# A mixture-of-experts pipeline with every handoff between engines a whole round apart, eight result buffers and scatters held for one round

## The chip, the core and the metric

The kernel runs on one core of one Trainium2 chip. The metric is the device time of the whole program in microseconds (us), median of several runs. The engines are TensorE (PE in the rows; PEld is its loading of weights), VectorE (DVE), ScalarE (ACT), GpSimd (POOL) and SyncE (SP, which here only issues DMAs).

## The reference

A small transformer block in float32 on `x` of shape (4, 256, 256). First `x` gets the result of a grouped-query attention (16 heads, 4 key/value heads, width 128, a causal mask and a learned bias) whose input is a gated bidirectional scan over the side input. Then `x` gets the result of a mixture of experts whose input is a second such scan `h`, flattened to 1024 tokens of width 256:

```python
logits = x @ gate_weight.T                       # 64 experts
routing_weights, selected = top_k(softmax(logits), 8)
routing_weights /= routing_weights.sum(-1)
for each expert e:
    gate, up = split(x @ gate_up_weights[e])     # 256 -> 2 x 96
    out = (silu(gate) * up) @ down_weights[e]    # 96 -> 256
    final += combine[:, e] * out
```

Each token goes to 8 of the 64 experts, so there are 8192 pairs of token and expert.

## The kernel before

The first some 320 us (attention, both scans, routing) are not touched by the change. At their end GpSimd has scattered each token's row of `h`, with its routing weight and its pair number, into a table in HBM (`slot_rows`), grouped by expert. What follows is the expert pipeline, then a fold that adds the eight results of every token.

**Tiles.** The pipeline works on 96 *doubles*. A double is 128 rows: two tiles of 64 rows, each with its own expert. The 32 fixed doubles cover the first 64 rows of every expert (expert 2j in the upper half, 2j+1 in the lower). The 64 extra doubles (28 to 91 in the order of work) take the rows beyond 64 of the experts that have them. Their experts are known only at run time, so their weights are read at an offset in a register, and those of the lower half are first copied to fixed places (`copy_gu` by VectorE, `copy_dn` by ScalarE).

**Groups and rounds.** Doubles 0 to 3 are groups of their own; from there on a group is two doubles and shares PSUM banks and evacuations. There are 50 groups. `ROUNDS` lists what a round works on: groups 0 to 3 singly, then two groups (four doubles) a round. There are NR = 27 rounds, of which 23 are full.

**The stages of a group**, with the semaphore that each hands on (in brackets):

1. SP loads the double's rows from `slot_rows` into one of ten `xrow` buffers, two DMAs a double (`rows_ld`). It may do so once VectorE has read the double ten before (`dest_ready`).
2. TensorE transposes the rows, `turn_rows` (`xt_done`); VectorE copies them from PSUM to `xg`, `copy_turned_rows` (`xt_copied`), and works out the weight column `wcol` and the row numbers `dest`, `find_rows` (`dest_ready`).
3. TensorE multiplies by the gate and up weights, `gate_up`, L1685 (`gu_done`).
4. ScalarE takes silu of the gate half into `sact`, `silu`, L833 (`silu_done`); VectorE multiplies by the up half and the routing weight into `aact`, `weigh`, L1323 (`act_ready`).
5. TensorE transposes `aact`, `turn_act` (`at_done`); ScalarE copies it to `aT`, `copy_turned` (`at_copied`).
6. TensorE multiplies by the down weights, `down`, L1706 (`dn_done`); ScalarE copies the result to `eout`, `copy_out` (`out_copied`).
7. GpSimd scatters `eout` to `pair_rows` in HBM with one indirect DMA for each double, L620 (`scattered[i]`, one semaphore for each of the six result buffers).

Every engine is in order, and each has its order written out by hand. In round `g` the orders are, where (g) stands for the groups of round g:

- TensorE: `turn_rows` (g), `turn_act` (g-2), `gate_up` (g-1), `down` (g-2).
- ScalarE: `copy_turned` (g-2), `silu` (g-1), `copy_out` (g-2), `copy_down` (g-1).
- VectorE: `copy_turned_rows` and `find_rows` (g), then `weigh` (g-1) and `copy_gate_up` (g) in turn, group by group.
- GpSimd follows `out_copied`, double by double.

So `weigh` of round g-2 ends while TensorE is near the end of its round g-1, and `turn_act` wants it after the eight transposes that begin round g; and `aT` is copied while TensorE does the `gate_up` that stands between `turn_act` and `down`. `sact` is one buffer: the second `silu` of a round waits for the first `weigh` (`act_ready`). The `gate_up` results use PSUM banks 2 and 3 in turn, the turned activations banks 4 and 5. Bank 5 is also used once, in round 5 (`TABLE_AT`), to turn the table of the extra doubles.

**The fold.** When the scatters have landed, SP loads `pair_rows` in eight slices of 1 MB (two DMAs each) into `pairs`, L472. VectorE adds half of each and TensorE the other half. Slices 0 and 1 wait for all scatters but those of the last three doubles:

```python
last = NDBL - TOPK // 2 + r // 2
for i in range(NOUT) if r == 0 else [last % NOUT]:
    sp.wait_ge(scattered[i], 16 * len(range(i, last + 1, NOUT)))
```

The functions that the change touches, and their callers:

## Time and profile before

| | |
|---|---|
| time, median of 3 runs | 521.24 us (520.41 to 523.81) |
| span of the profiled execution | 576.6 us |
| instructions in it | 10371 |
| TensorE busy in the span | 477.4 us (83%) |
| VectorE, ScalarE, GpSimd busy | 342.7, 305.9, 212.3 us |
| mean granted TensorE clock | 0.947 of full |

The profiled execution is 55.4 us longer than the median of the timed runs, with the same instructions. No time of its own is given for it beside its span. Starts in the rows are microseconds from the start of that span; durations of matmuls are modelled, their starts are recorded. The pipeline's full rounds lie between about 360 and 542 us of it.

### The profile page before, as it was taken

Reading aid. Unit: us, or ns where it says so; the run is one execution under the profiler, and the core shown is the slowest. Engines: PE = TensorE matmul, PEld = TensorE weight load, DVE = VectorE, ACT = ScalarE, POOL = GpSimd, SP = SyncE. Lnnn points to the kernel's source line nnn. Section 1 sums busy time; section 2 is a strip of 40 time slices with the busy share of each in tenths; the row PEclk is TensorE's granted clock in tenths of the full one; section 3 lists DMA queues with packets and bytes.
Section 4 is the critical chain, followed back from the end, with each engine's and each line's share of the span. In section 5 each row is a group of like instructions: output and inputs, shape, how many; then the busy total and the mean of one; then the engine's idle time right before and its main releaser. Section 6 shows DMA issues by size and latency. Waiting matters only on the chain. (4 is left out here: it accounts for less than half of the span.)

```text
span 576.6 us, 10371 instructions
## 1 busy us (share of the span) xinstructions
PE 477.4 (83%) x3073; PEld 351.1 (61%) x3073; DVE 342.7 (59%) x1204; ACT 305.9 (53%) x854; POOL 212.3 (37%) x224
## 2 busy tenths in 40 slices
PE   4586999999899899999983766987988888888666
PEld 1366767877787678788653423765665666655322
DVE  4768496596685894795793564544355454553033
ACT  3456787885966887779864201333244343444200
POOL 0344110041114631025584642245444455445600
PEclk9799999999999999999996788999899899899879
DMA  8920862000301102002998739884444444330097
GB/s 283 411 70 19 167 131 74 1 1 0 76 1 54 69 30 73 2 1 74 345 404 291 278 107 298 227 288 129 111 115 115 113 128 127 107 95 13 19 363 304
DMA packets 47318, 79.49 MB, mean 138 GB/s; under 512 B 8266, under 2 KB 31127, under 8 KB 46880
## 3 DMA queue, kind: packets, MB, share of 16 engines
q1 hardware_dynamic: 36864, 55.34, 31.1%
q0 software_dynamic: 7680, 16.93, 8.2%
q10 hardware_dynamic: 2720, 6.55, 3.5%
q8 instruction: 26, 0.43, 0.3%
q14 instruction: 28, 0.23, 0.1%
HBM read 56.54 MB, written 26.44 MB: 144 GB/s over the span
## 5 line engine op out<-in xcount | busy, mean ns | idle before, releaser
L620 POOL DMA_INDIRECT pair_rows<-eout,dest x93 | 91.8, 987 | 99.5 <-ACT eout L634 78.2
L833 ACT ACTIVATE sact<-ps 128x192 f32<-128x192 f32 (+1 forms) x50 | 16.3, 325 | 122.7 <-remote 73.6
L1323 DVE SCALAR_TENSOR_TENSOR aact<-sact,wcol,ps 128x96 f32<-128x96 f32 x96 | 26.0, 311 | 92.6 <-issue 87.1
L1685 PE MATMUL ps<-wts,xg 128*64 (+1 forms) x512 | 71.5, 342 | 3.7 <-DVE copy_gu L1346 2.2
L691 ACT ACTIVATE lg<-lg,mneg 128x128 f32<-128x128 f32 (+1 forms) x128 | 56.4, 443 | 26.1 <-DVE mneg L1029 21.5
L1685 PEld LDWEIGHTS ps<-wts,xg 128*64 128x64 f32 x512 | 53.0, 143 | 16.5 <-issue 9.5
L541 POOL DMA_INDIRECT slot_rows<-rows,pair_slot x48 | 47.9, 998 | 37.2 <-issue 24.1
L1512 PE MATMUL ps<-oT,wo_sb 128*128 128x256 f32 x240 | 54.4, 380 | 0.0
L1706 PE MATMUL ps<-wts,aT 96*64 96x256 f32 (+1 forms) x256 | 49.8, 395 | 4.4 <-issue 3.4
L1512 PEld LDWEIGHTS ps<-oT,wo_sb 128*128 128x128 f32 x240 | 44.6, 190 | 6.2 <-ACT oT L634 0.7
L634 ACT ACTIVATE lg<-lg,rinv 128x128 f32<-128x128 f32 (+1 forms) x128 | 45.9, 448 | 2.5 <-issue 1.7
L1685 PE MATMUL ps<-copy_gu,xg 128*64 128x192 f32 x256 | 46.6, 337 | 0.0
L1029 DVE CUSTOM_DVE_ANT_0 lg<-ps,bm 128x128 f32<-128x128 f32 (+1 forms) x128 | 36.9, 352 | 11.3 <-PE ps L1468 9.5
L1306 DVE COPY xg<-ps 128x512 f32<-128x512 f32 (+1 forms) x50 | 33.2, 664 | 15.4 <-PE ps L1387 8.8
L1387 PE MATMUL ps<-ident,xrow 128*128 128x128 f32 x192 | 31.0, 294 | 12.1 <-DMA xrow<-slot_rows 6.8
L1387 PEld LDWEIGHTS ps<-ident,xrow 128*128 128x128 f32 x192 | 22.3, 149 | 28.6 <-issue 21.2
L1383 PE MATMUL ps<-hh,wqh 128*128 128x256 f32 x128 | 38.1, 298 | 1.6 <-DVE kl L988 1.6
L1706 PE MATMUL ps<-copy_dn,aT 96*64 96x256 f32 x128 | 33.9, 385 | 6.4 <-issue 6.4
L1706 PEld LDWEIGHTS ps<-wts,aT 96*64 96x64 f32 x256 | 27.3, 141 | 15.8 <-issue 4.8
L1384 PE MATMUL ps<-hl,wqh 128*128 128x256 f32 x128 | 36.7, 287 | 0.0
L1385 PE MATMUL ps<-hh,wql 128*128 128x256 f32 x128 | 36.7, 287 | 0.0
L501 POOL TENSOR_TENSOR eukv<-euk,vT 128x512 f32<-128x512 f32 x8 | 10.2, 1273 | 67.1 <-ACT euk L669 50.6
(237 smaller groups left out, 1184.4 us busy)
## 6 DMA issues: line engine op xcount, KB each, us to landing
wts<-in_experts_dram SPq DMA_DIRECT2D x22, 640.0 KB, 8.0
xrow<-slot_rows SPq DMA_DIRECT2D x192, 65.0 KB
pairs<-pair_rows SPq DMA_DIRECT2D x16, 512.0 KB, 11.2
wts<-in_experts_dram ACTq DMA_DIRECT2D x10, 640.0 KB, 6.1
slot_rows<-zero SPq DMA_DIRECT2D x1, 4160.0 KB, 24.2
wT<-in_wq_t_dram SPq DMA_DIRECT2D x4, 512.0 KB, 6.5
wq_raw<-in_wq_l_dram SPq DMA_DIRECT2D x1, 2048.0 KB, 14.6
wo_sb<-in_wo_l_dram SPq DMA_DIRECT2D x1, 2048.0 KB, 20.5
```

The costliest lines, as they stand in the source:

```text
L541: nc.gpsimd.indirect_dma_start(out=slot_d, out_offset=bass.IndirectOffsetOnAxis(ap=pair_slot[:, t, k:k + 1], axis=0), in_=r[:, k, :], in_o ...
L620: nc.gpsimd.indirect_dma_start(out=pair_d, out_offset=bass.IndirectOffsetOnAxis(ap=dest[:, d:d + 1], axis=0), in_=out_rows(d), in_offset=N ...
L634: copy = lambda o_, i_, s=1.0: nc.scalar.activation(o_, i_, ACT.Copy, scale=s)
L691: ins = nc.scalar.activation(t, t, ACT.Exp, bias=mneg[:, u % 2, c:c + 1], scale=-1.0, accum_out=rsum[:, u % 2, c:c + 1])
L1029: ins = V.tensor_tensor_reduce(t, s, m, 1.0, FLT_BIG, ALU.add, ALU.min, mneg[:, u % 2, c:c + 1])
L1383: nc.tensor.matmul(o_, a[0], b_[0], start=start, stop=False)
L1384: nc.tensor.matmul(o_, a[0], b_[1], start=False, stop=False)
L1385: return nc.tensor.matmul(o_, a[1], b_[0], start=False, stop=stop)
L1387: T_ = lambda o_, i_, n=P: nc.tensor.transpose(o_, i_, ident[0:n, 0:n])
L1512: ins = nc.tensor.matmul(ps[:, 7, m * T:(m + 1) * T], wo_sb[:, n * G + h, m * P:(m + 1) * P], oT[:, h, :], start=(n == 0 and m == 0 and h ...
L1685: ins = nc.tensor.matmul(ps[h * R:(h + 1) * R, 2 + u % 2, k * I2:(k + 1) * I2], xg[u % len(xg)][:, k, cc, h * R:(h + 1) * R], moving, star ...
L1706: ins = nc.tensor.matmul(ps[h * R:(h + 1) * R, 6 + a % 2, k * C:(k + 1) * C], aT[a % 2][0:I, k, h * R:(h + 1) * R], moving, start=True, st ...
```

## The change

It alters only the expert pipeline.

- **TensorE** in round g: `turn_rows` (g) and `gate_up` (g-1) in turn, group by group; then `turn_act` (g-2); then `down` (g-3). The loop has one round more (NR + 3).
- **ScalarE** in round g: `silu` (g-1), `copy_turned` (g-2), `copy_down` (g-2), `copy_out` (g-3). `copy_turned` waits for both groups of its round.
- **VectorE** in round g: for each group `copy_turned_rows` and `copy_gate_up` (g), then `weigh` (g-1); both `find_rows` (g) at the end.
- **Buffers**: `sact` gets a second buffer; from group 8 on `gate_up` cycles through the three banks 5, 2, 3; both groups' turned activations share bank 4; the result buffers are eight (four pairs) and not six.
- **GpSimd**: in rounds 4 to 23 (`PACED`) the first scatter of round r waits until the down products of round r+1 are done.

```diff
-    NOUT = 6
+    NOUT = 8
@@
-        sact = at("sact", [P, 2, I], take(2 * I * 4))
+        sact = [at(f"sact{i}", [P, 2, I], off) for i, off in enumerate((take(2 * I * 4), row_off + 2 * KIB))]
@@
-        eout = at("eout", [P, NOUT, C], rows_off[0])
+        eout_pair = [at(f"eout{i}", [P, 2, C], off) for i, off in enumerate([rows_off[0] + 2 * i * KIB for i in range(NOUT // 2 - 1)] + [row_off])]
@@
+        PLAIN = 8
+        def gu_bank(u):
+            return 2 + u % 2 if u < PLAIN else (5, 2, 3)[(u - PLAIN) % 3]
+        def gu_before(u):
+            return u - 2 if u < PLAIN else u - 3
+        PACED = range(TOPK // 2, NR - 3)
@@ GpSimd
             for d in range(NDBL):
+                r = round_of[group_of[d]]
+                if r in PACED and group_of[d] == ROUNDS[r][0]:
+                    pool.wait_ge(dn_done, ROUNDS[r + 1][-1] + 1)
                 pool.wait_ge(out_copied, group_of[d] + 1)
@@ ScalarE, copy_turned and silu
-                act.wait_ge(at_done, a + 1)
+                act.wait_ge(at_done, ROUNDS[round_of[a]][-1] + 1)
@@
-                if u >= 1:
-                    act.wait_ge(act_ready, u)
+                if u >= 2:
+                    act.wait_ge(act_ready, u - 1)
@@ ScalarE, the loop
-            for g in range(NR + 2):
+            for g in range(NR + 3):
                 us = ROUNDS[g - 1] if 1 <= g <= NR else []
-                outs = ROUNDS[g - 2] if g >= 2 else []
-                for a in outs:
-                    copy_turned(a)
+                outs = ROUNDS[g - 2] if 2 <= g < NR + 2 else []
                 for u in us:
                     silu(u)
                 for a in outs:
+                    copy_turned(a)
+                for a in outs:
+                    copy_down(a)
+                for a in ROUNDS[g - 3] if g >= 3 else []:
                     copy_out(a)
-                for u in us:
-                    copy_down(u)
@@ VectorE, the loop
-                for x in ins_:
-                    copy_turned_rows(x)
-                    find_rows(x)
                 us = ROUNDS[g - 1] if g else []
                 for k in range(max(len(us), len(ins_))):
+                    if k < len(ins_):
+                        copy_turned_rows(ins_[k])
+                        copy_gate_up(ins_[k])
                     if k < len(us):
                         dve.wait_ge(dest_ready, us[k] + 1)
                         weigh(us[k])
-                    if k < len(ins_):
-                        copy_gate_up(ins_[k])
+                for x in ins_:
+                    find_rows(x)
@@ TensorE, turn_act and gate_up
-                if a >= 2:
-                    pe.wait_ge(at_copied, a - 1)
-                if a == TABLE_AT:
-                    pe.wait_ge(cols_read, 2)
+                if a == ROUNDS[round_of[a]][0] and a:
+                    pe.wait_ge(at_copied, a)
@@
-                if u >= 2:
-                    pe.wait_ge(act_ready, u - 1)
+                if u == PLAIN:
+                    pe.wait_ge(cols_read, 2)
+                if gu_before(u) >= 0:
+                    pe.wait_ge(act_ready, gu_before(u) + 1)
@@ TensorE, the loop
-            for g in range(NR + 2):
-                outs = ROUNDS[g - 2] if g >= 2 else []
+            for g in range(NR + 3):
                 if g < len(IDLE):
                     keep_clock(IDLE[g])
-                for x in ROUNDS[g] if g < NR else []:
-                    turn_rows(x)
-                for a in outs:
+                xs = ROUNDS[g] if g < NR else []
+                us = ROUNDS[g - 1] if 1 <= g <= NR else []
+                for k in range(max(len(xs), len(us))):
+                    if k < len(xs):
+                        turn_rows(xs[k])
+                    if k < len(us):
+                        gate_up(us[k])
+                for a in ROUNDS[g - 2] if 2 <= g < NR + 2 else []:
                     turn_act(a)
-                for u in ROUNDS[g - 1] if 1 <= g <= NR else []:
-                    gate_up(u)
-                for a in outs:
+                for a in ROUNDS[g - 3] if g >= 3 else []:
                     down(a)
```

## Rows read from the trace of the kernel before

**Rows 1.** The page: span, and TensorE's busy tenths in 40 slices

```profile
span 576.6 us, 10371 instructions
PE   4586999999899899999983766987988888888666
```

**Rows 2.** Stretches: us, then busy us of PE, PEld, DVE, ACT, POOL; clock; DMA share; GB/s

```profile
410.00:508.50 98.50, 84.00 (x721) 60.09 (x722) 49.14 (x216) 40.83 (x121) 47.47 (x48) 0.97 0.43 119
...
544.50:577.00 32.50, 18.06 (x33) 6.24 (x32) 9.80 (x8) 1.19 (x2) 3.94 (x4) 0.89 0.80 303
```

**Rows 3.** Groups of instructions in 410.0 to 508.5 us: busy, mean ns, idle before

```profile
L620 POOL DMA_INDIRECT pair_rows<-eout,dest x48 | 47.5, 989 | 51.3 <-ACT eout L634 40.3 <-issue 11.0
L1323 DVE SCALAR_TENSOR_TENSOR aact<-sact,wcol,ps 128x96 f32<-128x96 f32 x48 | 12.9, 311 | 47.8 <-issue 47.8
L833 ACT ACTIVATE sact<-ps 128x192 f32<-128x192 f32 x25 | 8.3, 331 | 57.4 <-remote 32.9 <-PE ps L1685 9.6 <-issue 8.4
```

**Rows 4.** Timeline of round 6 and the start of 7 (TensorE, then ScalarE): start, us, what, idle before

```profile
365.01 1.04 PE L1387 MATMUL ps<-ident,xrow 128*128 128x128 f32 x8
366.94 2.82 PE L1685 MATMUL ps<-wts,xg 128*64 128x192 f32 x32
369.60 1.90 PE L1706 MATMUL ps<-wts,aT 96*64 96x256 f32 x16
371.43 1.09 PE L1387 MATMUL ps<-ident,xrow 128*128 128x128 f32 x8
...
368.51 0.33 ACT L833 ACTIVATE sact<-ps 128x192 f32<-128x192 f32 x1 [1.08 <-PE ps L1685]
```

**Rows 5.** Timeline of round 20 by engine: TensorE, ScalarE, VectorE

```profile
475.03 1.09 PE L1387 MATMUL ps<-ident,xrow 128*128 128x128 f32 x8
475.96 0.60 PE L1387 MATMUL ps<-ident,aact 128*96 128x128 f32 x4
...
479.14 0.38 PE L1706 MATMUL ps<-wts,aT 96*64 x1
...
481.14 0.33 PE L1387 MATMUL ps<-ident,xrow 128*128 128x128 f32 x1
...
477.35 0.65 ACT L634 ACTIVATE aT<-ps 96x256 f32<-96x256 f32 x2
480.80 0.33 ACT L833 ACTIVATE sact<-ps 128x192 f32<-128x192 f32 x1 [2.80 <-PE ps L1685]
...
481.21 0.54 DVE L1323 SCALAR_TENSOR_TENSOR aact<-sact,wcol,ps 128x96 f32<-128x96 f32 x2 [2.82 <-issue]
```

**Rows 6.** Round 20's gate and up products alone: us, PE busy, PEld busy

```profile
476.49:479.14 2.65, 2.65 (x32) 2.21 (x32) 1.00 0.37 97
```

**Rows 7.** Timeline of GpSimd from 522 us: the scatters of rounds 23 to 26

```profile
524.89 0.98 POOL L620 DMA_INDIRECT pair_rows<-eout,dest  x1 [2.50 <-ACT eout L634]
532.24 0.98 POOL L620 DMA_INDIRECT pair_rows<-eout,dest  x1 [2.50 <-ACT eout L634]
...
539.34 0.98 POOL L620 DMA_INDIRECT pair_rows<-eout,dest  x1 [2.25 <-ACT eout L634]
...
544.50 0.98 POOL L620 DMA_INDIRECT pair_rows<-eout,dest  x1 [0.30 <-issue]
...
548.37 0.98 POOL L620 DMA_INDIRECT pair_rows<-eout,dest  x1 [0.30 <-issue]
```

**Rows 8.** Timeline from 522 us: SP's queue, then TensorE's start of round 26

```profile
547.08 10.13 SPq L472 DMA_DIRECT2D pairs<-pair_rows  x16
...
522.28 0.55 PE L1387 MATMUL ps<-ident,xrow 128*128 128x128 f32 x3
```

**Rows 9.** The chain that ended last: the last scatter's landing

```profile
547.08 6.20 DMA pair_rows<-eout,dest
```

**Rows 10.** Waits of SP's queue in 395 to 545 us: total, times, longest

```profile
SPq L429 <- DVE dest L1314: 10.1, 6, 2.7
```

**Rows 11.** Timeline of TensorE in the single rounds

```profile
354.05 0.44 PE L1387 MATMUL ps<-ident,xrow 128*128 128x128 f32 x2 [2.38 <-DMA xrow<-slot_rows]
```

More of the change, by code:

```diff
@@ L214, in adaln_attn_ffn @@
         o = 16 * KIB
-        xg = [at(f"xg{i}", [P, 2, CC, P], off) for i, off in enumerate((take(2 * KIB), take(2 * KIB), r3 + 10 * KIB, rows_off[0] + NOUT * KIB))]
+        xg = [at(f"xg{i}", [P, 2, CC, P], off) for i, off in enumerate((take(2 * KIB), take(2 * KIB), r3 + 10 * KIB, rows_off[0] + (NOUT - 2) * KIB))]
         wcol = at("wcol", [P, (NE + MORE) // 2], take(384))
-        sact = at("sact", [P, 2, I], take(2 * I * 4))
+        sact = [at(f"sact{i}", [P, 2, I], off) for i, off in enumerate((take(2 * I * 4), row_off + 2 * KIB))]
         aact0 = take(2 * I * 4)
@@ L358, in adaln_attn_ffn @@
         NR = len(ROUNDS)
+        round_of = {g: r for r, gs in enumerate(ROUNDS) for g in gs}
         TABLE_AT = 5
@@ L830, in silu @@
                 act.wait_ge(gu_done, u + 1)
-                if u >= 1:
-                    act.wait_ge(act_ready, u)
-                nc.scalar.activation(sact[:, 0:n, :], ps[:, 2 + u % 2, 0:n * I2].rearrange("p (k i) -> p k i", k=n)[:, :, 0:I],
+                if u >= 2:
+                    act.wait_ge(act_ready, u - 1)
+                nc.scalar.activation(sact[u % 2][:, 0:n, :], ps[:, gu_bank(u), 0:n * I2].rearrange("p (k i) -> p k i", k=n)[:, :, 0:I],
                                      ACT.Silu).then_inc(silu_done, 1)
@@ L845, in copy_out @@
                 else:
-                    copy(eout[:, d % NOUT:d % NOUT + n, :], ps[:, 6 + a % 2, 0:n * C].rearrange("p (k c) -> p k c", k=n)
+                    copy(eout_pair[d % NOUT // 2][:], ps[:, 6 + a % 2, 0:n * C].rearrange("p (k c) -> p k c", k=n)
                          ).then_inc(out_copied, 1)
@@ L1322, in weigh @@
                 for k, d in enumerate(GROUPS[u]):
-                    ins = V.scalar_tensor_tensor(out=aact[u % 2][:, k, :], in0=sact[:, k, :], scalar=wcol[:, d:d + 1],
-                                                 in1=ps[:, 2 + u % 2, k * I2 + I:(k + 1) * I2], op0=ALU.mult, op1=ALU.mult)
+                    ins = V.scalar_tensor_tensor(out=aact[u % 2][:, k, :], in0=sact[u % 2][:, k, :], scalar=wcol[:, d:d + 1],
+                                                 in1=ps[:, gu_bank(u), k * I2 + I:(k + 1) * I2], op0=ALU.mult, op1=ALU.mult)
                 ins.then_inc(act_ready, 1)
@@ L1684, in gate_up @@
                                 moving = copy_gu[m % NCOPY][:, cc * I2:(cc + 1) * I2]
-                            ins = nc.tensor.matmul(ps[h * R:(h + 1) * R, 2 + u % 2, k * I2:(k + 1) * I2],
+                            ins = nc.tensor.matmul(ps[h * R:(h + 1) * R, gu_bank(u), k * I2:(k + 1) * I2],
                                                    xg[u % len(xg)][:, k, cc, h * R:(h + 1) * R], moving, start=(cc == 0), stop=(cc == CC - 1))
```

7 lines of the change are left out of this document (3 added, 4 removed).

## The prediction

> **What bounds the kernel now.** The page comes first: in the pipeline's part of the span, from slice 26 on, TensorE is busy eight to nine tenths, a little less than before it [rows 1]. The stretches put numbers to it. Twelve full rounds with extra experts take 98.5 us, so 8.21 us each; in them TensorE is busy 84.0 / 12 = 7.0 us, VectorE 4.1, ScalarE 3.4, GpSimd 4.0 [rows 2]. From the start of round 6 (365.01) to that of round 26 (522.28) there are 20 rounds in 157.3 us, 7.86 each [rows 4, 8]. No other engine comes near that time, so what can be won is TensorE's own waiting.
>
> How long must a round be? Rounds 6 and 20 give the pieces by their starts: eight row transposes 475.03 to 475.96, 0.93 us; four transposes of activations to 476.49, 0.53; 32 gate and up records 2.65; 16 down records 479.14 to 481.14, 2.00 (1.83 in round 6, 369.60 to the next start at 371.43). Together 5.9 to 6.1 us [rows 4 to 6]. So the profiled round holds 7.86 - 6.0 = 1.9 us of stall, and over the 20 rounds and the last ones (21 in all) that is 39 us. This is the most that a better order can give.
>
> Then I asked what the stall is. In round 6 silu begins at 368.51, 1.57 us after `gate_up` began (366.94): half of the 2.82 us, plus a hop [rows 4]. In round 20 the same silu begins at 480.80, 4.31 us after 476.49, though ScalarE had been idle 2.80 us and the products had the same length; the releaser named is the product itself [rows 5, 6]. The matmul is recorded as run and its signal comes some 2.9 us late. VectorE then idles as long (2.82 us before L1323), which is where nearly all of its 47.8 us at that line and ScalarE's 57.4 at L833 come from [rows 3, 5]. So the handoff that is late in this trace is the completion of a dense run of matmuls, and not `turn_act` waiting for a slow VectorE.
>
> Is that lateness there when nobody records? The recorder writes every instruction, and a full round has 60 matmul and 60 weight-load records, the densest stretch of the program. The profiled execution is 55.4 us longer than the median. If the timed rounds take 6.1 us, 21 x 1.75 = 37 us of it lie here, and 18 are left for the rest. If the timed rounds were as long as the profiled ones, all 55 us would have to come out of the other 410, much of which TensorE fills to eight or nine tenths [rows 1]. I take the first: in the timed runs a round is already about 6.1 us, and TensorE is nearly full. This is argued, not seen, and it is the largest choice here.
>
> **The change part by part.** *Order of TensorE, `sact`, banks.* These take the short handoffs away: `turn_act` no longer waits for the second `weigh`, `gate_up` waits for an `act_ready` one group older, the two silus do not wait for each other. Worth: between 0 (no stall in a timed round) and 1.9 us a round. Would a round of 6.0 us have stalled before? With TensorE at t = 0: the gate and up products of the first group end at 0.93 + 0.53 + 1.33 = 2.8, silu takes 0.33 and `weigh` 0.54 with hops of about 0.25, so 4.2; the second silu can go at 4.5, its `weigh` ends by 5.7; `turn_act` wants it at 6.0 + 0.93 = 6.9. Slack 1.2 us. The copy to `aT` (0.65) starts at 1.8 and `down` wants it at 4.1: slack 1.6. VectorE's 4.1 us and ScalarE's 3.4 fit in 6.0. So I put the saving in a timed round at 0.1 to 0.15 us, for rounds that a late DMA or a fall of the clock (0.97 in the extra rounds) [rows 2] puts out of step: 21 x 0.13 = 2.7 us, bounds 0 and 39.
>
> *VectorE's order.* The four `find_rows` pairs move behind both `weigh`, about 2.5 us later. SP is queued behind them: its loads wait for `dest_ready`. Today that wait is 10.1 us in six places over some 18 rounds [rows 10], and SP's eight DMAs a round run about a round ahead of their use (round 20's are issued while round 18 runs). The 2.5 us come out of that lead: 0, or up to 0.3 us a round if SP falls behind, 6 us.
>
> *ScalarE's order.* `copy_down` waits for the down products four doubles back, then `copy_out` for dn_done and for scatters two rounds old; silu of the next round is queued behind both. It has a round of slack now: 0.
>
> *Filling the pipeline.* In rounds 1 to 5 TensorE waits for the rows' DMAs (2.38 us at 354.05) [rows 11], and the stage that is one round deeper hides there: 0, bound 1 us.
>
> *The hold and the deeper drain.* This has a price that I can count. Before, the scatters of round r follow `down` (r), which TensorE does in its round r+2. After, `down` (r) is in round r+3 and its scatters wait for `down` (r+1), in round r+4: two rounds later. In the middle nothing waits for them (the eight buffers see to it), but GpSimd is the last to finish, and it can't catch up: an indirect DMA holds it for (548.37 - 544.50) / 3 = 1.29 us, 5.16 us a round [rows 7]. At the end of TensorE's round 26 GpSimd before starts on round 24, after on round 22. `PACED` ends at 23, so from there both run without a pause, and after has 8 scatters more before it: 8 x 1.29 = 10.3 us. The fold hangs on this: SP's first load of `pairs` is issued at 547.08, 2.58 us after double 92's scatter began, and the fold then takes 29.5 us to the end of the span, with its DMAs 80% busy [rows 2, 7, 8]. Nothing there gets shorter; the last scatter lands at 553.28, 4.9 us after its issue, well inside the loads [rows 7, 9].
>
> For a timed round of 6.0, with S the start of round 26: before, scatters of 24 can start at S + 6.2, and double 92's at S + 6.2 + 10.3 = S + 16.5. After, those of 22 start at S + 6.3 and double 92's at S + 6.3 + 16 x 1.29 = S + 26.9. Cost 10.4 us. In the profiled rounds GpSimd had pauses of 2.25 to 2.50 us left before each of its last three rounds, and double 92 started at S + 22.2; after: round 26 done at S + 8, so S + 8.3 + 20.6 = S + 28.9, cost 6.7 [rows 7, 8]. Bounds 5 and 12.
>
> **Sum.** Timed: -2.7 + 10.4 = +7.7, about +7: **528 us**. For the profiled execution, whose completions come no faster than 60 matmuls in about 7.3 us (the last rounds' first scatters at 524.89, 532.24 and 539.34, 7.35 and 7.10 apart) [rows 7]: 21 x (7.86 - 7.45) = -8.6, +6.7, so its span stays near 576.6, perhaps 575. I expect the two to differ in this way.
>
> **A rule from the skill.** The last rounds have no row loads and still take 7.1 to 7.35 us [rows 7]. The Trainium skill, page "TensorE: Matmul & The Clock Gate", section "Wait — 56ns, not 53.3ns?", says that without hardware decoding the sequencer spends about 62 ns on every MATMUL. If weight loads cost the same, 120 x 62 ns = 7.4 us would be the least that a round can take, timed or not; an estimate from that page. The trace speaks against it as the cause: 64 records pass in 2.65 us, 41 ns each [rows 6]. By that rule the result is the second case below.
>
> **The rivals.** *Second case: TensorE has a floor of some 7.4 us a round in timed runs too.* A limit on how fast matmuls complete, and not the recorder, then makes the 7.1 to 7.35 us of the last rounds. Before loses what stands over it, 21 x 0.45 = 9.5 us, mostly in rounds with extra experts (8.21 us). After wins 9.5 and pays 7 to 10: 518 to 522, say 520. For it: the steady pace; against it: round 6, with 6.42 us to the next start.
>
> *Third case: the stalls are real and all go.* If a timed round takes 7.2 us now (7.86 x 521/577), it falls to 6.1: -23, +10: 508, and 495 at the far end. For it: the large idle sums of rows 3. Against it: the slack worked out above.
>
> *Fourth case: the hold becomes the bound.* `copy_out` of round r+2 needs the scatters of round r, which start 0.2 us after `dn_done` (r+1); the last starts 3.9 us later and lands after 2.6 to 4.9 us more, so 6.7 to 9.0; a copy (0.6) and the down products (1.0) close the loop at 8.5 to 11 us, with 12 us (two rounds) to spend. It decides once landings pass some 9 us, or if ScalarE, held there, makes silu late. Then 0.3 to 0.5 us a round, +8 more: 536.
>
> *The change doesn't do what it says*: the second case is that too, for the order of TensorE would be changed and its pace not.
>
> **How the numbers follow.** First case 0.46, around 528, itself 525 to 531. Second 0.25. Third 0.16. Fourth 0.13. About 1% (5.2 us) is what a measurement here tells from no change. Slower by over 1% (above 526.5): 0.13 + 0.35 of the first = 0.48. Faster (below 516): the third, and 0.05 of the second = 0.21. Within: 0.31. For 8 in 10 the range leaves out the lower two thirds of the third case and the upper part of the fourth: 511 to 535. More chance lies above no change than below.
>
> **What would show it.** The GpSimd row of round 23 waits for `down` (24); from there about 16 scatters stand 1.29 apart without a gap, and SP's first load of `pairs` comes some 31 us after TensorE starts round 26, where it was 24.8. The idle time before L1387's transposes of `aact` is gone. If the rounds of the changed profile go on at 7.3 to 7.5 us, completion sets the pace, by recorder or by chip, and the silu rows still stand 3 us behind their products. A round near 6.0 in the profile would refute my reading and bring the third case. The prediction is wrong too if the timed rounds held a stall that this trace can't show, or if GpSimd's 1.29 us is shorter when nothing is recorded: at 1.0 the tail costs 8 and not 10.3.

## The result and the profile after

| | before | after |
|---|---|---|
| time, median | 521.4 us (520.41 to 523.81, 4 runs) | 539.57 us (538.78 to 543.99, 4 runs) |
| ratio | | 1.0323, 95% interval 1.0251 to 1.0394 |
| span of the profiled execution | 576.6, and 522.8 when taken again | 537.0 |
| own time of that execution | none given, and 524.62 | 538.78 |

The change makes the kernel 3.2% slower, beyond the upper end of the forecast. The execution behind the first trace was about 55 us longer than the median of the timed ones; the unchanged kernel, profiled again (`before_again` below), has a trace like its timed runs, and everything from here on compares with that one.

The page of after: span, TensorE's busy tenths, granted clock in tenths.

```profile
span 537.0 us, 10348 instructions
PE   4786999999999799989989685999999999997375
PEclk9899999999999999999999779899999999997669
```

TensorE is full from slice 26 to 36, as in [rows 1] it was not. The stretches of after: TensorE's rounds 12 to 25; from there to SP's first load of `pairs`; the fold. Columns as in [rows 2].

```profile
385.07:476.44 91.37, 91.37 (x843) 61.70 (x841) 59.14 (x254) 48.60 (x136) 55.79 (x56) 1.00 0.52 147
476.44:507.16 30.72, 22.46 (x154) 13.23 (x152) 4.98 (x28) 12.71 (x33) 21.80 (x23) 0.79 0.07 21
507.16:537.00 29.84, 17.74 (x32) 6.47 (x32) 9.80 (x8) 1.20 (x2) 1.88 (x2) 0.82 0.87 327
```

The same three stretches of the kernel before, second trace.

```profile
390.42:473.57 83.15, 83.15 (x842) 64.81 (x840) 60.58 (x252) 51.23 (x140) 55.55 (x56) 1.00 0.54 153
473.57:493.02 19.45, 15.49 (x138) 10.50 (x136) 4.21 (x19) 9.55 (x25) 13.79 (x14) 0.98 0.04 7
493.02:522.80 29.78, 17.37 (x32) 6.06 (x32) 9.80 (x8) 1.19 (x2) 1.97 (x2) 0.84 0.87 327
```

In the first stretch TensorE is busy all of the time in both kernels, at the full clock (1.00, the level of 2.4 GHz), with the same matmuls (843 and 842 records), and yet it is 8.2 us longer: 14 rounds of 6.53 us where there were 14 of 5.94. The second is 11.3 us longer, the fold the same. Ahead of round 12 after wins 3.9 us, from `keep_clock` (310.60 and 312.07) to round 12 (385.07 and 390.42), and 1.5 more in code that the change doesn't touch. Sum: -1.5 - 3.9 + 8.2 + 11.3 + 0.1 = 14.2 us, the difference of the two spans. The medians are 18 apart; the start of `keep_clock` alone lay between 310.60 and 316.24 us in fourteen traces (all but the first), ahead of any edit, so some us between a trace and a median say nothing.

The granted clock of the second stretch, 0.79 against 0.98, isn't what makes it longer: in after it falls 14.4 us behind the start of round 26, when GpSimd's last scatters have been running without a pause for 7 us (below).

**TensorE's round.** Timeline of round 18 of after, the start of each run of equal work:

```profile
424.22 0.66 PE L1401 MATMUL ps<-ident,xrow 128*128 128x128 f32 x4
424.81 0.38 PE L1699 MATMUL ps<-wts,xg 128*64 x1
...
426.26 0.66 PE L1401 MATMUL ps<-ident,xrow 128*128 128x128 f32 x4
426.85 0.38 PE L1699 MATMUL ps<-wts,xg 128*64 x1
...
428.30 0.64 PE L1401 MATMUL ps<-ident,aact 128*96 128x128 f32 x4
428.87 0.43 PE L1720 MATMUL ps<-wts,aT 96*64 x1
...
430.75 0.66 PE L1401 MATMUL ps<-ident,xrow 128*128 128x128 f32 x4
```

And of the kernel before, second trace, the same round:

```profile
426.06 1.09 PE L1387 MATMUL ps<-ident,xrow 128*128 128x128 f32 x8
426.99 0.60 PE L1387 MATMUL ps<-ident,aact 128*96 128x128 f32 x4
427.52 0.38 PE L1685 MATMUL ps<-wts,xg 128*64 x1
...
430.17 0.38 PE L1706 MATMUL ps<-wts,aT 96*64 x1
...
430.39 0.38 PE L1706 MATMUL ps<-wts,aT 96*64 x1
...
432.00 1.09 PE L1387 MATMUL ps<-ident,xrow 128*128 128x128 f32 x8
```

Read the starts. Before: 0.93 + 0.53 + 2.65 + 1.83 = 5.94. After: 0.59 + 1.45 + 0.59 + 1.45 + 0.57 + 1.88 = 6.53. The twelve transposes take 1.75 us in three parts and 1.46 in one; the 32 gate and up records 2.90 in two parts and 2.65 in one. No idle time is marked at any of these rows, since the modelled ends of matmuls (0.66 for a group that hands over after 0.59) cover it. The pitch of the starts shows the loss.

TensorE's weight loads (PEld) show it too, at the same places. Round 18 of after:

```profile
424.81 0.13 PEld L1699 LDWEIGHTS ps<-wts,xg 128*64 128x64 f32 x1 [0.17 <-issue]
426.26 0.42 PEld L1401 LDWEIGHTS ps<-ident,xrow 128*128 128x128 f32 x4 [0.28 <-issue]
426.85 0.13 PEld L1699 LDWEIGHTS ps<-wts,xg 128*64 128x64 f32 x1 [0.17 <-issue]
```

At each change of kind the loads stop, for 0.17 to 0.39 us, and go on at the very start of the new kind's first matmul; inside a run they begin ahead of it (in before's round 18 the first load for `aact` at 426.88, its matmul at 426.99). In the 14 rounds the loads stop 28 times before (two a round, 7.9 us in all) and 84 times in after (six a round, 20.4 us). Most have the mark `issue`: no semaphore is seen that held them.

The handoff that the first trace showed late is not late here. ScalarE's `silu` of before, second trace, to be held against the 2.80 us and the start 4.31 us after `gate_up` of [rows 5]: it starts 1.57 us after 427.52.

```profile
429.09 0.33 ACT L833 ACTIVATE sact<-ps 128x192 f32<-128x192 f32 x1 [0.34 <-PE ps L1685]
430.39 0.33 ACT L833 ACTIVATE sact<-ps 128x192 f32<-128x192 f32 x1 [0.97 <-PE ps L1685]
```

**The scatters.** GpSimd's timeline in after: the first held scatter of round 22 (double 76), the next, and double 92's.

```profile
483.82 0.98 POOL L634 DMA_INDIRECT pair_rows<-eout,dest  x1 [1.67 <-PE ps L1720]
485.11 0.99 POOL L634 DMA_INDIRECT pair_rows<-eout,dest  x1 [0.30 <-issue]
...
504.48 0.99 POOL L634 DMA_INDIRECT pair_rows<-eout,dest  x1 [0.30 <-issue]
```

In before, second trace, the first scatter of round 23 (double 80) and double 92's:

```profile
474.19 0.98 POOL L620 DMA_INDIRECT pair_rows<-eout,dest  x1 [1.06 <-ACT eout L634]
...
490.45 0.98 POOL L620 DMA_INDIRECT pair_rows<-eout,dest  x1 [0.30 <-issue]
```

After: double 76 goes at S + 7.4 (S is the start of TensorE's round 26), the sixteenth behind it, double 92, at S + 28.0, with no pause between. Before: S + 16.9. That is what the forecast worked out from [rows 7], and nearly its numbers (S + 26.9 and S + 16.5). SP's first load of `pairs` follows 2.6 to 2.7 us later in both.

### The profile page after: what moved, and what is told of

It is laid out like the page before. It is cut to its first block, busy times and chain, and to the rows that moved or that the text cites. A ratio compares the mean times of both kernels' runs of the same rounds, so it can differ in the third digit from the quotient of the medians.

```text
span 537.0 us, 10348 instructions
## 1 busy us (share of the span) xinstructions
PE 472.4 (88%) x3073; PEld 338.5 (63%) x3073; DVE 343.0 (64%) x1204; ACT 308.7 (57%) x854; POOL 214.1 (40%) x224
## 4 chain that ended last, share of the span: by engine, by line
PE 55%; DVE 14%; ACT 14%; DMA 7%; issue 5%; POOL 4%; SPq 0%; POOLq 0%; ACTq 0%; DVEq 0%
PE ps L1699 13%; PE ps L1401 10%; PE ps L1720 8%; PE ps L1526 6%; ACT lg L705 4%; DVE lg L1043 3%; ACT lg L648 3%; DMA pairs<-pair_rows 3%; POOL slot_rows L624 2%; PE ps L1397 2%; PE ps L1399 2%; PE ps L1398 2%; PE ps L1449 2%; POOL pair_rows L634 2%; PE ps L1442 2%
## 5 line engine op out<-in xcount | busy, mean ns | idle before, releaser
L1699 PE MATMUL ps<-wts,xg 128*64 (+1 forms) x512 | 74.3, 339 | 0.5 <-DVE xg L1320 0.5
L1699 PEld LDWEIGHTS ps<-wts,xg 128*64 128x64 f32 x512 | 49.9, 139 | 14.8 <-issue 7.8
L1720 PE MATMUL ps<-wts,aT 96*64 96x256 f32 (+1 forms) x256 | 50.9, 413 | 2.2 <-issue 1.1
L1699 PE MATMUL ps<-copy_gu,xg 128*64 128x192 f32 x256 | 48.5, 332 | 0.0
L1320 DVE COPY xg<-ps 128x512 f32<-128x512 f32 (+1 forms) x50 | 33.1, 662 | 15.6 <-PE ps L1401 15.5
L648 ACT ACTIVATE aT<-ps 96x256 f32<-96x256 f32 (+1 forms) x50 | 18.6, 372 | 41.0 <-PE ps L1720 40.2
L1401 PE MATMUL ps<-ident,xrow 128*128 128x128 f32 x192 | 32.5, 291 | 6.7 <-DMA xrow<-slot_rows 6.7
L1720 PEld LDWEIGHTS ps<-wts,aT 96*64 96x64 f32 x256 | 25.8, 145 | 18.8 <-issue 7.5
L1401 PEld LDWEIGHTS ps<-ident,xrow 128*128 128x128 f32 x192 | 20.6, 143 | 25.2 <-issue 21.5
L518 POOL TENSOR_TENSOR df<-df,euk 128x512 f32<-128x512 f32 x7 | 8.9, 1277 | 67.2 <-DVE df L984 67.2
## 6 DMA issues: line engine op xcount, KB each, us to landing
wts<-in_experts_dram SPq DMA_DIRECT2D x22, 640.0 KB, 14.4
```

The source lines that it names most:

```text
L648: copy = lambda o_, i_, s=1.0: nc.scalar.activation(o_, i_, ACT.Copy, scale=s)
L1401: T_ = lambda o_, i_, n=P: nc.tensor.transpose(o_, i_, ident[0:n, 0:n])
L1699: ins = nc.tensor.matmul(ps[h * R:(h + 1) * R, gu_bank(u), k * I2:(k + 1) * I2], xg[u % len(xg)][:, k, cc, h * R:(h + 1) * R], moving, sta ...
L1720: ins = nc.tensor.matmul(ps[h * R:(h + 1) * R, 6 + a % 2, k * C:(k + 1) * C], aT[a % 2][0:I, k, h * R:(h + 1) * R], moving, start=True, st ...
```

## The experiments

Each trace is read in three stretches: A, from the start of `keep_clock` to that of TensorE's round 12 (the single rounds and the first full ones); R, the 14 rounds from there to the start of round 26; and D, from there to SP's first load of `pairs`. An *excursion* is each time that TensorE goes from transposes to products and back in a round. A, R and D come from one trace each; the time is the median of 4 to 12 runs, and the ratio compares them with runs of the kernel before on the same chip (before, taken again: one run).

| kernel | A | R | D | time, ratio (95%) |
|---|---|---|---|---|
| before, taken again | 78.35 | 83.15 | 19.45 | 524.62 |
| after | 74.47 | 91.37 | 30.72 | 539.57, 1.032 (1.025 to 1.039) |
| `e1_no_hold` | 74.32 | 91.37 | 28.14 | 537.5, 1.025 (1.018 to 1.033) |
| `e2_rows_first` | 75.44 | 88.22 | 30.40 | 538.63, 1.027 (1.018 to 1.035) |
| `e4_turns_together` | 77.42 | 86.40 | 30.67 | 539.25, 1.028 (1.020 to 1.036) |
| `e3_together_no_hold` | 77.77 | 85.95 | 27.68 | 534.44, 1.020 (1.012 to 1.028) |
| `e6_copy_out_first` | 74.55 | 85.76 | 26.47 | 532.6, 1.018 (1.010 to 1.026) |
| `e8_find_rows_early` | 75.43 | 84.74 | 26.47 | 531.52, 1.017 (1.012 to 1.023) |
| `e5_before_interleaved` | 76.4 | 87.4 | 19.77 | 528.1, 1.008 (1.004 to 1.011) |
| `e7_before_early_apart` | 75.42 | 83.15 | 19.46 | 524.84, 0.998 (0.994 to 1.002) |
| `e9_before_find_rows_late` | 77.95 | 84.23 | 19.47 | 528.8, 1.009 (1.005 to 1.014) |
| `e10_before_two_sact` | 77.85 | 83.15 | 19.46 | 524.57, 1.001 (0.997 to 1.005) |
| `e11_before_hold` | 76.28 | 85.89 | 25.43 | 531.22, 1.014 (1.008 to 1.021) |
| `e12_before_four_apart` | 81.73 | 97.60 | 20.52 | 542.97, 1.037 (1.032 to 1.042) |

A scatters by 3 to 4 us between kernels that hardly differ (77.77 and 74.55 for `e3` and `e6`). It hangs on when the first rows land, and on the granted clock: in all traces the clock is at half (0.5, 1.2 GHz) for a while in the first rounds, and in `before_again`, `e3`, `e4`, `e10` and `e12` once more, for 3.4 us somewhere between 351 and 390 us. Five of the six longest A are theirs (77.4 to 81.7; the sixth is `e9`), the others have 74.3 to 76.4. In `before_again` it comes in round 6, behind a stretch in which TensorE had waited for rows, and its gate and up products take 4.01 us there where they take 2.65. R is at the full clock in every one of these traces. R and D repeat to 0.1 us where nothing is changed.

### The kernel before, taken again

No edit.

> The kernel before, unchanged, for a trace of an execution that takes the time of the timed runs. The one trace of it so far spans 576.6 us against a median of 521.4; the changed kernel's trace spans 537.0 against 539.6 timed. If the long trace was one slow execution, this one spans about 520, a full round of TensorE takes 5.9 to 6.1 us, silu starts within 0.3 us of its product's end, and the first row transposes of the pipeline begin some 14 us earlier. If the recorder itself slows this kernel, it spans 570 to 580 again.

Its time was 524.62 us, its span 522.8; 14 full rounds of exactly 5.94 us without a wait of TensorE, and `silu` 0.3 us behind its product. A profile is taken here too, so the recorder does not make completions late; the first trace showed a disturbed execution. Of the 53.8 us between the two traces, 13.0 lie ahead of `keep_clock`, 6.5 in A, 29.3 in R and 5.4 in D: the disturbance was not the pipeline's alone. Two things in this document's forecast were read off it and are wrong for the kernel: the lateness, and SP's distance ahead of TensorE (below).

### Without the hold

```diff
-        PACED = range(TOPK // 2, NR - 3)
+        PACED = range(0)
```

> The changed kernel without the hold of the scatters (all rounds free). Theory: the drain is one round deeper anyway, so the last scatters wait for the last down products and the gain is less than the hold's 10.3 us: double 92's scatter moves from 28.0 us after the start of round 26 to about 21.6, so 6.4 us less, 533 us. Rival (the prediction's term): the whole 10.3 us come back, 529. Rival 2: the hold costs nothing because copies and buffers pace the scatters, 539. The rounds stay at 6.52 us in all three.

D falls by 2.6 us, less than either gain that was thought of (6.4 and 10.3), and the rounds stay at 6.53. So by the traces the hold is a fifth of the change's cost (14.2); the ratios, 1.025 and 1.032, overlap and can't confirm it alone. GpSimd's first scatter of round 23 (double 80), 10.0 us after round 26 began (477.92); in after it went at 488.99, 12.5 us after:

```profile
487.91 0.98 POOL L634 DMA_INDIRECT pair_rows<-eout,dest  x1 [2.10 <-ACT eout L648]
```

### TensorE's order

In after, both `turn_rows` ahead of both `gate_up` (four runs of work a round):

```diff
-                for k in range(max(len(xs), len(us))):
-                    if k < len(xs):
-                        turn_rows(xs[k])
-                    if k < len(us):
-                        gate_up(us[k])
+                for x in xs:
+                    turn_rows(x)
+                for u in us:
+                    gate_up(u)
```

> The changed kernel, with TensorE doing both row transposes of a round and then both gate and up products, as before, and the rest of the change kept. Theory: each change of kind on TensorE (transposes to products and back) costs 0.11 to 0.17 us; the changed kernel has six in a round, this one four, so a round falls from 6.52 to about 6.25 us and the time by 23 x 0.27 = 6 us, to 533.5. Rival: TensorE's round is 6.52 for another reason (weights, dispatch, VectorE), and the order changes nothing, 539.

A round is 1.03 + 2.75 + 0.57 + 1.88 = 6.23 us, 0.30 less, and 0.285 more than before's. (R holds another 1.1 us of waits ahead of `gate_up`.) The round is as expected, the time is not: 538.63 and not 533.5. In the traces R is 3.2 us shorter than in after, A 1.0 longer and `keep_clock` 2.9 later.

In the kernel before, `turn_rows` and `gate_up` interleaved and nothing else:

```diff
-                for x in ROUNDS[g] if g < NR else []:
-                    turn_rows(x)
-                for a in outs:
-                    turn_act(a)
-                for u in ROUNDS[g - 1] if 1 <= g <= NR else []:
-                    gate_up(u)
...
+                for k in range(max(len(xs), len(us))):
+                    if k < len(xs):
+                        turn_rows(xs[k])
+                    if k == 0:
+                        for a in outs:
+                            turn_act(a)
+                    if k < len(us):
+                        gate_up(us[k])
...
```

> The kernel before with one edit: TensorE does the second group's row transposes after the first group's gate and up products. Changes of kind go from three to five in a round. Theory: 2 x 0.13 x 23 = 6 us slower, 527. Rival: the cost of the changed kernel lies in its drain and hold alone, and this stays at 521.

6.24 us a round: again 0.30, without the deeper pipeline. Interleaving costs by itself, in the timed runs too: 1.008 (1.004 to 1.011), 2.3 to 5.7 us.

In after, `turn_act` behind both `turn_rows`, then both `gate_up`: before's kinds of work in before's order.

```diff
-                for k in range(max(len(xs), len(us))):
-                    if k < len(xs):
-                        turn_rows(xs[k])
-                    if k < len(us):
-                        gate_up(us[k])
+                for x in xs:
+                    turn_rows(x)
                 for a in ROUNDS[g - 2] if 2 <= g < NR + 2 else []:
                     turn_act(a)
+                for u in us:
+                    gate_up(u)
```

> The changed kernel with one edit: TensorE does both row transposes, then the transposes of activations, then both gate and up products, then the down products (three changes of kind in a round, as before the change); depth, buffers and hold stay. Theory: the 0.585 us that a round has grown (6.525 against 5.94 in the undisturbed trace of before) are three more changes of kind and nothing else, so the full rounds fall to about 5.94 and the time by 20 x 0.585 = 11.7 us, to 528. Rival: half of it belongs to the deeper pipeline (e2, with four changes, fell to 6.23 but its time hardly moved: new waits of TensorE on the scatters' chain took it back); then the rounds show gaps and the time stays above 533.

Rounds without a wait take 5.94 us: one excursion, one excursion's time, with the deeper pipeline in place. But R is 3.25 us above before's: TensorE now waits for loads of rows (2.2 us in five of the rounds) and ahead of `gate_up` (1.1 us). Its timeline at round 24 of this kernel; the last double's loads landed at 466.34:

```profile
464.79 0.88 PE L1401 MATMUL ps<-ident,xrow 128*128 128x128 f32 x6
466.39 0.44 PE L1401 MATMUL ps<-ident,xrow 128*128 128x128 f32 x2 [0.72 <-DMA xrow<-slot_rows]
```

The time is that of after and not the expected 528, although R is 5.0 us shorter: in this trace A is 3.0 longer than after's (with the third stretch at half clock), and the start of `keep_clock` was 3.3 us later for reasons ahead of the edit. Four timed runs can't part these, so that the order's 5 us reach the time is not shown by this pair; `e5` and `e12` show it.

The same without the hold (`PACED = range(0)`, as above):

> e4 without the hold. Theory: the hold itself is worth 2.5 us at the end (e1: double 92's scatter at 25.5 us after the start of round 26 against 28.0), since without it the copy of the results still stands last in ScalarE's round: 526. If the hold also causes TensorE's occasional waits once the round is shorter than 6.5 us (seen in e2), more comes back here: 523 to 525.

D is 3.0 us shorter than with the hold (2.5 expected), and the time 534.44 (526 expected): order and hold together give back some 5 us of the medians, though the intervals of the ratios, 1.012 to 1.028 and 1.025 to 1.039, overlap a little.

### Is it the alternation or a handoff?

All of this could still be a handoff between groups. So the kernel before was cut finer: two row transposes, then eight gate and up records, four times a round, with the same instructions and waits.

```diff
...
+                    for i in range(4):
+                        if i:
+                            turn_rows(xs[i // 2], (i % 2,))
+                        gate_up(us[i // 2], (i % 2,))
...
```

> The kernel before with TensorE's full rounds cut finer: two row transposes and then eight gate and up records, four times a round (the four transposes of activations stand with the first two), so that a round goes from transposes to products and back four times instead of once. Nothing else is changed, every instruction and wait is the same. Theory A (each going from transposes to column-tiled products and back costs about 0.29 us, whatever waits stand there: one excursion more gave 0.285 and 0.30, two more gave 0.585): three more give 0.88, a round of 6.8 us, 95.4 us for the 14 rounds from 12 to 26, and about 16 us more in all, ratio 1.03. Rival B (the 0.3 us are the handoff between groups, a semaphore's round trip or a bank, paid once a group): no more than the 6.24 us of the order with one excursion more, ratio 1.007 to 1.01.

R is 97.6 us, 6.97 a round: 6.85 and 7.11 in turn (406.96 to 413.81 is one of the short; every second one holds some 0.2 us of wait). Expected was 6.8. One excursion from transposes to products and back, from its timeline:

```profile
410.65 0.33 PE L1690 MATMUL ps<-copy_gu,xg 128*64 128x192 f32 x1
410.91 0.44 PE L1387 MATMUL ps<-ident,xrow 128*128 128x128 f32 x2
411.27 0.38 PE L1690 MATMUL ps<-wts,xg 128*64 x1
411.28 0.38 PE L1690 MATMUL ps<-copy_gu,xg 128*64 128x192 f32 x1
411.49 0.33 PE L1690 MATMUL ps<-wts,xg 128*64 x1
```

Pairs of product records stand 0.16 us apart in a run, but 0.26 into the transposes; two transposes take 0.23 (0.93 / 4) in a run and 0.36 here; the first pair has 0.22 to the next and not 0.16. 0.10 + 0.13 + 0.06 = 0.29 us, at a place where no wait is recorded. With one, two and four excursions a round takes 5.94, 6.24 (6.23 in the changed kernel) and 6.85, with three (after) 6.53: a straight line of 0.3 us each. The stops of the weight loads go along: two a round in before, four in `e2` and `e5`, six in after, eight here. And the time follows: 1.037 (1.032 to 1.042), against 1.007 to 1.01 for a cost paid once a group. From gate and up to down products, both of 64 columns, nothing is lost.

### ScalarE's order

`e3_together_no_hold` with `copy_out` (g-3) ahead of `copy_down` (g-2).

```diff
+                for a in ROUNDS[g - 3] if g >= 3 else []:
+                    copy_out(a)
                 for a in outs:
                     copy_down(a)
-                for a in ROUNDS[g - 3] if g >= 3 else []:
-                    copy_out(a)
```

> e3 with the result copies ahead of copy_down on ScalarE. Theory: what is left of the tail is one round of depth (four scatters, 5.2 us) and the late place of copy_out (3.2 us, 487.9 against a possible 484.7 in e1); this gives the second back: double 92's scatter at 22 to 22.5 us after the start of round 26, 3 us less than e3, 523. Rival: copy_down, now later, makes the down products wait, and the rounds grow: 526 or more.

D falls by 1.2 us (3 expected), for `copy_down` (1.33 us for its four copies) no longer stands between the last round's down products and their scatters. The time fell by 1.8, within what the intervals leave open.

### VectorE's order

`e6_copy_out_first` with `find_rows` back behind each `copy_turned_rows`:

```diff
                     if k < len(ins_):
                         copy_turned_rows(ins_[k])
+                        find_rows(ins_[k])
                         copy_gate_up(ins_[k])
@@
-                for x in ins_:
-                    find_rows(x)
```

> The changed kernel with turn_rows and turn_act together, no hold, copy_out ahead of copy_down, and VectorE's find_rows back right behind copy_turned_rows. Theory A (the late find_rows costs SP its lead, and that is what makes TensorE wait for rows in the last full rounds): the waits for xrow go, the 14 rounds from 12 to 26 take 5.94 us each, 83.2 us, against 85.8 us with find_rows late, and the time falls from 532.6 to about 530 us. Rival B (SP is full anyway, the lead is lost to the deeper pipeline or to TensorE's order): the waits stay, about 532.5 us. In both, what is left over the kernel before (521 to 526) is the drain, S26 to SP's first load of pairs 26.5 us and not 19.5, less what the first rounds win.

R is 1.0 us shorter and not 2.6. The waits for `xrow` are gone but for one of 0.2 us; others of 0.1 to 0.4 us ahead of `gate_up` stay (1.3 us in 14 rounds), which before doesn't have. They stand in every second round; what makes them was not tried. The times, 531.52 and 532.6, each beside its own runs of the kernel before, can't tell.

The same edit the other way round, in the kernel before:

```diff
                 for x in ins_:
                     copy_turned_rows(x)
-                    find_rows(x)
@@
                     if k < len(ins_):
                         copy_gate_up(ins_[k])
+                for x in ins_:
+                    find_rows(x)
```

> The kernel before with one edit: find_rows of both groups at the end of VectorE's round, behind weigh and copy_gate_up. Theory A (SP has about 1.8 us of lead left in the late rounds, find_rows moves some 2.5 us later): 0.1 to 0.2 us a round in the 14 rounds from 12 to 26 as waits of the row transposes for xrow, 2 to 3 us in all, ratio 1.004 to 1.006. Rival B (SP's DMA issues alone set its pace, whatever VectorE does): no change, the 14 rounds again 83.2 us.

R is 1.1 us longer, the time by 2.7 to 7 us; the profile shows less than the expected 2 to 3 and the timed runs more, and I can't say why they differ. SP's waits for `dest` in the whole trace rise from 2.9 us to 6.9 (after: 7.0), and its lead is used up: in before's second trace the last double of round 24 lands 1.8 us ahead of the round, here TensorE's loading of weights (PEld) waits for it.

```profile
463.87 0.20 PEld L1388 LDWEIGHTS ps<-ident,xrow 128*128 128x128 f32 x2 [0.24 <-DMA xrow<-slot_rows]
```

### A second sact buffer in the kernel before

```diff
-                if u >= 1:
-                    act.wait_ge(act_ready, u)
+                if u >= 2:
+                    act.wait_ge(act_ready, u - 1)
```

(with `sact[u % 2]` where `sact` was)

> The kernel before with one edit: a second sact buffer, so that the second silu of a round waits for a weigh one group older. Theory A (no handoff cost anything before, rounds 12 to 26 run at 5.94 us with TensorE never waiting): no change within 0.3%, the 14 rounds 83.2 us. Rival B (the first rounds, where TensorE stood still for some 5 us, stalled at this handoff): a gain of 1 to 3 us ahead of round 12.

1.001 (0.997 to 1.005), R 83.15 to the hundredth. The handoff that it relaxes cost nothing.

### The hold alone in the kernel before

Eight buffers (as in the change) and the hold, in before's order of everything.

```diff
-    NOUT = 6
+    NOUT = 8
...
             for d in range(NDBL):
+                r = round_of[group_of[d]]
+                if r in PACED and group_of[d] == ROUNDS[r][0]:
+                    pool.wait_ge(dn_done, ROUNDS[r + 1][-1] + 1)
```

> The kernel before with the hold alone: eight result buffers, and in rounds 4 to 23 the first scatter of a round waits for the next round's down products. TensorE's order is that of before. Theory A (the hold costs only where it delays the first scatter of the last held round, after which 16 scatters stand 1.29 us apart): before, double 92's scatter began 16.9 us after round 26; held, the first scatter of round 23 goes at 6.1 us after it and double 92's at 6.1 + 15.5 = 21.6, so +4.7 us, ratio 1.009, and the rounds stay at 5.94. Rival B (the hold costs what it cost in the changed kernel, 2.6 to 3.0 us): ratio 1.005. Rival C (eight buffers and the hold also disturb the rounds, through copy_out waiting for landings): over 6 us.

D is 6.0 us longer (expected 4.7, and 2.6 to 3.0 by the rival), R another 2.7. Most of D is the hold itself, as expected: the first scatter of round 23 waits for the down products of round 24 and the fifteen behind it follow without a pause. But it goes 7.3 us after the start of round 26 and not 6.1. Some 0.5 of that is a late `down` in round 26 (it begins 3.08 us after gate and up and not 2.65). This and R's 2.7 have the cause that the forecast named in its fourth case: `copy_out` waits for scatters of two rounds ago, and what is queued behind it on ScalarE is late. First the sums of ScalarE's and TensorE's waits over R and D (total, times, longest), then one of them in ScalarE's timeline:

```profile
ACT eout L639 <- DMA pair_rows<-eout,dest: 26.2, 18, 3.1
...
PE ps L1711 <- ACT aT L639: 4.1, 4, 2.1
```

```profile
414.61 0.60 ACT L639 ACTIVATE eout<-ps 128x512 f32<-128x512 f32 x1 [3.03 <-DMA pair_rows<-eout,dest]
415.11 1.32 ACT L639 ACTIVATE copy_dn<-wts 96x256 f32 x4
416.33 0.63 ACT L639 ACTIVATE aT<-ps 96x256 f32<-96x256 f32 x2
```

26.2 us in 18 waits, and behind the one shown `aT` is copied late and `down` waits 1.1 us. In after `copy_out` stands last in its round with a round more to spend: in R it waits 0.4 us for a scatter, once, and TensorE never waits for it. The kernel before has the same loss once, in its round 8 (second trace):

```profile
368.27 0.60 ACT L634 ACTIVATE eout<-ps 128x512 f32<-128x512 f32 x1 [3.70 <-DMA pair_rows<-eout,dest]
```

Gate and up to down takes 3.56 us in that round and not 2.65.

### Interleaving only where rows are late

If interleaving hides late loads in the first full rounds, it should be used there alone: the kernel before, with one `turn_rows` and one `gate_up` ahead of the rest in rounds 5 and 6.

```diff
...
+                apart = g in (5, 6)
+                if apart:
+                    turn_rows(xs[0])
+                    gate_up(us[0])
+                for x in xs[apart:]:
...
-                for u in ROUNDS[g - 1] if 1 <= g <= NR else []:
+                for u in us[apart:]:
```

> The kernel before with TensorE interleaving row transposes and gate and up products in rounds 5 and 6 alone. The undisturbed trace of before loses about 5 us in rounds 5 to 11 that the changed kernel doesn't: 0.93 and 1.07 us of waiting for row loads in round 6 and then a gate and up run at half clock (4.19 us for 2.82). Theory: the interleaved order has products to do while rows land, so most of that 3.4 us comes back: 520.5 against 523.4 (ratio 0.995). Rival: the rows land no earlier and TensorE waits elsewhere, 523.4.

0.998 (0.994 to 1.002), where 0.995 was expected: A is 2.9 us shorter in the trace (and without the third stretch at half clock), which is no more than its scatter, and the timed runs show no gain that can be told. It is the best of all these kernels, and not shown to be better than before.

## Why the prediction was wrong

**The step that failed** is the first term of the sum, "Order of TensorE, `sact`, banks", put at -2.7 us with bounds 0 and 39 us of gain. It counted the waits that the order takes away and took the records' own time for fixed, so the bound was 0 on the side of a loss, where there was no reason for one. What the runs showed: each further change between transposes and products costs 0.15 us, an excursion 0.3; after has two excursions more, 0.585 us a round, 8.2 us in R and more in the rounds around it. So the term was +8.2 or more and not -2.7, 10.9 of the 11.6 us by which 528 was short. `e5_before_interleaved` and `e12_before_four_apart` show it without any other part of the change. A warning stood in the starts even before: a pair of down records takes 0.21 us (430.17 to 430.39 above), so eight pairs 1.7, while the next transposes begin 1.83 after the first, in round 6 too [rows 4]. I took the 1.83 us for the records' own time and never asked what stood in the 0.13 us behind the eight pairs.

**That a timed round is about 6.1 us already** was right (5.94), and so was that the order has no stall to win in the full rounds: `e10_before_two_sact` gives nothing and no wait of a matmul stands in 14 rounds. The reason given was wrong. I blamed the recorder; the second trace was recorded as well, its rounds from 12 on have no late completion, and they are the densest of all, 120 records in 5.94 us. What disturbed the first execution stays open. It matters for the forecast of the profiled execution (575): it was 537.0.

**The hold and the deeper drain**, +10.4, bounds 5 and 12: measured 11.2 for double 92's start, 11.3 for D. Mechanism and place are right. The division was off: not a round of scatters each. Along `e6`, `e3`, `e1` and after, D goes 26.47, 27.68, 28.14, 30.72 from before's 19.45: 1.2 us for `copy_out` behind `copy_down`, 0.5 for the longer rounds, 2.6 for the hold, since without it the scatters of round 23 wait for `copy_out` anyway. The first 7.0 us, before to `e6`, are what is left of the change when these are out; that they are the deeper pipeline is read from the place of the scatters (the first of round 23 goes 0.6 us after the start of round 26 in before, 7.7 in `e6`); no run has the depth alone.

**ScalarE's order at 0** was off by that 1.2 us: a round of slack in the middle is none at the end, where the last copies are on the way to the last scatters.

**VectorE's order**, 0 to 6 us from SP's lead of "about a round": right in kind. The lead was read off the disturbed execution. Undisturbed the last loads of a round land 4.9 us ahead of it in round 12 and 1.8 us in round 24, since SP takes 6.2 us for a round's eight loads and TensorE 5.94. In after no matmul waits for rows in R: its rounds are longer, and interleaved it needs the last double 2.3 us into the round and not 0.7. In `e4` and `e9` the wait appears.

**Filling, 0 to 1 us**: A was 3.9 us shorter in after's trace. TensorE's waits for `xrow` in it fell from 8.9 us in six to 6.7 in three, as would be if products of the round before filled the time until the second group's rows land. But A scatters by as much, `e6` has 74.55 without interleaving, and `e7` gained nothing in its timed runs. Two pieces of it are before's own losses that after's trace doesn't have: 1.4 us of gate and up products at half clock in round 6, and 0.9 us in round 8, where `copy_out` waited for a scatter. How much of the 3.9 is the change's stays open.

**The rivals.** The second needed a floor of 7.4 us a round: gone, 120 records pass in 5.94 us, 49.5 ns each, and not the 62 that the forecast's estimate took for weight loads too. The Trainium skill (page "TensorE: Matmul & The Clock Gate", section "Wait — 56ns, not 53.3ns?") has about 62 ns for each MATMUL, without hardware decoding, and no such figure for weight loads. The runs don't contradict that: a round's 60 matmuls alone have 99 ns each. The third needed stalls: gone. (Its start has a slip: 7.86 x 521/577 is 7.1 and not 7.2, so the case gives 510 and not 508.) The fourth, 536, came nearest in time (3.6 us off), yet for a reason that didn't occur in after (no wait of TensorE for it); its mechanism is real and shows in `e11`, where the pipeline is one round shallower.

The forecast's own sum, 521.2 + 7.7, is 528.9, written as 528. The sum as it should have stood, from the traces: +8.2 and +11.3, less 0 to 3.9 ahead of round 12: 15.6 to 19.5 us. The medians give 18.2.

## What to carry to other kernels

A reordering is not free on an engine that is full: here each further change between the two kinds of matmul cost 0.15 us. Count the changes, look at the pitch of starts across one in the trace of before (and at the stops of the weight loads), and give the term a bound on the side of a loss. Where every engine's pace hangs on a pipeline, one round more of depth is paid at its end by whoever is last there, and the end is where slack found in the middle doesn't hold. And if a profiled execution is a tenth longer than the timed ones, waits and leads read from it are not the kernel's: read from it only what does not depend on them, such as the spacing of scatters.

## What the chip showed unexpectedly

- Going from 128x128 float32 transposes to matmuls of 64 columns that run in pairs and back costs 0.29 us (0.10 into the transposes, 0.13 around two of them, 0.06 behind), with no wait of a matmul recorded; three more such excursions a round made 5.94 into 6.85 us. The weight loads stop at each such change, 0.17 or 0.18 us into the products and 0.28 to 0.39 us into the transposes in after's rounds. Why they stop was not tried.
- TensorE passed 120 records (60 matmuls and 60 weight loads) in 5.94 us, round after round.
- One execution of the kernel before, of more than sixty, was 10% longer than the rest. 13.0 us of the 53.8 were lost ahead of the pipeline; in it `silu` starts 1.8 to 5.2 us behind the last product's start from about 374 us on, for nearly every group, where it is 0.37 for nearly all in the second trace. The granted clock in its rounds was 0.97 and not 1.00 [rows 2], which is too little for it: 3% of 8 us is 0.2, and the rounds are 2 us longer.
